# A four-layer transformer kernel: token rows go to fixed expert regions in bursts of four scatters, with gathers and maxima moved

## The chip, the cores and the metric

The kernel runs on one core of a Trainium2 chip. The metric is the device time of one execution in microseconds (us). Engines are named as the profile names them: PE (matrix products, with PEld for its weight loads), DVE (vector), ACT (activations, and one DMA queue), POOL (elementwise work and the indirect DMAs), SP (only a DMA queue).

## The reference

Eight sequences of 256 tokens with 128 features pass four layers, each added to its input. The two `ffn` layers share their weights.

```python
x = x + attn_a(layernorm(x))   # "rope": 16 heads of 8, rotated q, k, v; output rotated back
x = x + ffn(layernorm(x))      # "ffn"
x = x + attn_b(layernorm(x))   # "cov": covariance scores of centred heads
x = x + ffn(layernorm(x))      # "ffn"
# ffn(x): h = x + attention(ln1(x)); h + moe(ln2(h))
# moe(t): probs = softmax(t @ w_gate); top 2 of 8 experts, weights renormalised
#         out += we[:, None] * (gelu(t @ w1[e] + b1[e]) @ w2[e] + b2[e])     # 128 -> 512 -> 128
```

## The kernel before

All activations stay in SBUF: `X` and `Hs` (residual streams), `U` (normed input of the mixture). Two phases (`ph` 0 and 1) each hold an attention layer (rope, then cov) and an ffn layer. A phase is a software pipeline of `STEPS` = 21 steps. In step `s` six sequences are in different stages, oldest first: `u` (gate), `t` (output projection), `a` (scores and values), `m` (row maxima), `n` (projection and stacking), `p` (norm). So step 18 is the last in which scores are made, and steps 19 and 20 are drained inside the mixture. Each engine runs its own hand-written order of these parts (`step` in each engine's block); counting semaphores join them. PSUM has a ring of four banks that ACT reads (`bankE`), three that DVE reads (`bankR`) and one for values (`bankO`).

The attention part: PE makes raw scores into `bankR`, DVE takes maxima of them (`do_max`, L1109, two heads at a time), then scores go into `bankE`, ACT exponentiates (L834) and PE multiplies with the values (L466). For the rope layer DVE makes two products per tensor (`rotate`, L1093) that POOL adds (`rotated`), for keys, queries and values. POOL norms a sequence (`norm`), and stacks keys and queries in split precision (`stack_k`, `stack_q`).

The mixture: after the attention of an ffn layer, tokens are sorted by expert, in two halves of four sequences, since each token goes to two experts. DVE chooses experts (`choose`, `weigh`), PE counts (`do_rank`), and DVE works out from counts and ranks (`sort_rows`) the place of each token's two rows in a list in which each expert has whole tiles of 128 rows (`SLOT`), and each tile's expert (`EID`). A half has `NTL` = 23 tiles. POOL writes `U` to these places in DRAM (`scatter`, L1560: 16 indirect DMAs of 128 rows of 512 bytes per half, in one run: the first half's after step 18, the second's after step 20). SP loads each tile's first-layer weights (`load_w`, L393 reads the expert's number into a register, L395 loads 258 KB; seven buffers) and groups of four sorted tiles (`load_x`, L384, 256 KB; two buffers). PE turns a group (`turn_x`, L695), then for each tile multiplies into 512 hidden features (`hidden`, L707) and back (`outputs`, L720); ACT applies gelu (L951), DVE copies out (`evacuate`, L1312), ACT's queue stores to `sorted_y` (L962). Later POOL fetches each token's two rows (`gather`, L1578) into eight buffers `Yg`, and DVE adds them with their weights (`combine`, L1323). In PE's order `turn_x` of a half's first two groups stands ahead of its first `hidden`, and `hidden` runs three tiles ahead of `outputs`. `drain` puts the end of the ffn attention's work beside the tiles of the first half, and `fill` the start of the cov layer beside the second half of phase 0. Phase 1 has no `fill`: its second half is tiles alone, then gathers and the output.

Before all this SP writes zeros over `sorted_u` once (L367), since places without a token are read too.

## Time and profile before

| | |
|---|---|
| time, median of 3 runs | 901.24 us (893.77 to 902.31) |
| the profiled execution | 898.2 us, its span 896.4 us |
| granted clock of PE, mean of the span | 0.923 |
| busy: PE, PEld, DVE, ACT, POOL | 86%, 61%, 61%, 61%, 54% |
| phase 0: steps / mixture | to about 297 us / 323 to about 460 us |
| phase 1: steps / mixture, end | to about 725 us / 754 to 896 us |

A line of the profile names the source line, the engine, the operation and its operands (out<-in), how often it stands there in a row (x8), and in brackets how long the engine had been idle and what ended that. The clock is given in shares of full speed; it has two levels, 1.00 and 0.50.

### The profile page before, as it was taken

Reading aid. Unit: us, or ns where it says so; the run is one execution under the profiler, and the core shown is the slowest. Engines: PE = TensorE matmul, PEld = TensorE weight load, DVE = VectorE, ACT = ScalarE, POOL = GpSimd, SP = SyncE. Lnnn points to the kernel's source line nnn. Section 1 sums busy time; section 2 is a strip of 40 time slices with the busy share of each in tenths; the row PEclk is TensorE's granted clock in tenths of the full one; section 3 lists DMA queues with packets and bytes.
Section 4 is the critical chain, followed back from the end, with each engine's and each line's share of the span. In section 5 each row is a group of like instructions: output and inputs, shape, how many; then the busy total and the mean of one; then the engine's idle time right before and its main releaser. Section 6 shows DMA issues by size and latency. Waiting matters only on the chain.

```text
span 896.4 us, 21301 instructions
## 1 busy us (share of the span) xinstructions
PE 767.0 (86%) x7166; PEld 546.7 (61%) x7166; DVE 544.5 (61%) x1370; ACT 543.4 (61%) x1264; POOL 484.2 (54%) x906
## 2 busy tenths in 40 slices
PE   1999999999999399697988999999999948968970
PEld 1756655666565189497964565566666525958970
DVE  4699899788988123012486887878889822211232
ACT  0377777878787256154546676787877834715640
POOL 6667678747762621504645665844777273060436
PEclk9999999999999789698999899999999977978995
DMA  9300000000000436266210000000000042635842
GB/s 274 111 3 3 3 2 3 4 3 3 4 2 4 130 107 175 79 182 175 79 38 13 16 18 5 4 3 3 3 3 3 3 124 77 173 103 143 245 124 67
DMA packets 57657, 56.29 MB, mean 63 GB/s; under 512 B 6856, under 2 KB 42448, under 8 KB 57552
## 3 DMA queue, kind: packets, MB, share of 16 engines
q1 hardware_dynamic: 39200, 39.13, 15.5%
q0 software_dynamic: 4096, 8.40, 3.2%
q10 hardware_dynamic: 14256, 7.41, 2.9%
q8 instruction: 61, 1.00, 0.5%
q14 instruction: 44, 0.36, 0.1%
HBM read 40.10 MB, written 14.29 MB: 61 GB/s over the span
## 4 chain that ended last, share of the span: by engine, by line
PE 56%; DVE 21%; issue 11%; POOL 7%; DMA 3%; ACT 2%; another core or an unknown queue 0%; ACTq 0%; POOLq 0%; DVEq 0%; SPq 0%
DVE M L1109 11%; PE bankO L466 11%; PE bankR L720 8%; PE bankE L707 7%; PE bankE L485 7%; PE bankE L439 6%; DVE QKV L1071 2%; POOL Yg L1578 2%; PE bankR L452 2%; PE bankE L476 2%; PE bankR L506 2%; PE bankR L536 1%; PE bankR L738 1%; PE bankR L554 1%; DMA Yg<-sorted_y,SLOT 1%
## 5 line engine op out<-in xcount | busy, mean ns | idle before, releaser
L1109 DVE TENSOR_REDUCE M<-bankR 128x2 f32<-128x512 f32 x512 | 326.4, 684 | 62.7 <-PE bankR L452 56.9
L834 ACT ACTIVATE Pr<-bankE 128x512 f32<-128x512 f32 x512 | 277.7, 595 | 129.5 <-PE bankE L439 109.1
L466 PE MATMUL bankO<-Pr,Vx 128*32 128x256 f32 x2048 | 170.5, 406 | 18.8 <-issue 16.1
L452 PE MATMUL bankR<-KQ 32*128 32x256 f32 x1024 | 171.3, 339 | 5.0 <-DVE M L1109 2.9
L439 PEld LDWEIGHTS bankE<-KQ 32*128 32x128 f32 x1024 | 79.6, 188 | 97.1 <-issue 64.2
L439 PE MATMUL bankE<-KQ 32*128 32x256 f32 x1024 | 133.3, 335 | 0.5 <-issue 0.5
L1312 DVE COPY Yb<-bankR 128x128 f32<-128x128 f32 x92 | 26.4, 290 | 167.9 <-PE bankR L720 111.1
L452 PEld LDWEIGHTS bankR<-KQ 32*128 32x128 f32 x1024 | 110.1, 191 | 17.1 <-DVE M L1109 12.8
L951 ACT ACTIVATE G<-bankE,W 128x128 f32<-128x128 f32 x368 | 101.5, 384 | 24.8 <-PE bankE L707 14.0
L707 PE MATMUL bankE<-XTT,W 128*128 128x128 f32 x736 | 105.1, 288 | 11.4 <-issue 4.6
L1578 POOL DMA_INDIRECT Yg<-sorted_y,SLOT x64 | 62.2, 971 | 95.6 <-DMA sorted_y<-Yb 42.0
L720 PE MATMUL bankR<-w,G 128*128 x736 | 102.7, 284 | 8.6 <-issue 6.3
L1560 POOL DMA_INDIRECT sorted_u<-U,SLOT x64 | 62.2, 972 | 80.2 <-DVE past L1292 61.9
L707 PEld LDWEIGHTS bankE<-XTT,W 128*128 128x128 f32 x736 | 95.0, 201 | 16.1 <-issue 10.8
L720 PEld LDWEIGHTS bankR<-w,G 128*128 128x128 f32 x736 | 93.4, 198 | 11.4 <-issue 11.0
L828 ACT ACTIVATE KQ<-bankE 128x512 fp32r<-128x512 f32 x128 | 70.5, 605 | 24.7 <-PE bankE L485 24.4
L466 PEld LDWEIGHTS bankO<-Pr,Vx 128*32 128x32 f32 x2048 | 41.2, 110 | 55.7 <-issue 30.2
L942 ACT ACTIVATE XTT<-bankE,lncols 128x512 f32<-128x512 f32 (+1 forms) x24 | 18.3, 763 | 68.2 <-PE bankE L695 35.9
L1402 POOL TENSOR_SCALAR lnsmall<-meanvar 128x2 f32<-128x2 f32 x48 | 11.1, 232 | 83.5 <-DVE meanvar L1039 80.9
L1477 POOL CAST Kst<-QKV 128x512 fp32r<-128x512 f32 x24 | 15.7, 654 | 65.0 <-DVE QKV L1071 37.5
L485 PE MATMUL bankE<-ident_r,Kst 128*128 128x256 f32 (+1 forms) x256 | 39.9, 302 | 4.1 <-POOL Kst L1480 4.1
L1323 DVE SCALAR_TENSOR_TENSOR X<-Yg,SH,X 128x128 f32<-128x128 f32 x64 | 22.3, 362 | 33.6 <-DMA Yg<-sorted_y,SLOT 30.0
(169 smaller groups left out, 1147.0 us busy)
## 6 DMA issues: line engine op xcount, KB each, us to landing
W<-in_w1b SPq DMA_DIRECT2D x92, 258.0 KB
sorted_y<-Yb ACTq DMA_DIRECT2D x92, 64.0 KB
XT<-sorted_u SPq DMA_DIRECT2D x20, 256.0 KB
sorted_u<-Yg SPq DMA_DIRECT2D x2, 1472.0 KB, 9.7
KQ<-MT SPq DMA_DIRECT2D x128, 4.0 KB
X<-in_x SPq DMA_DIRECT2D x8, 128.0 KB, 7.3
sorted_u<-U,SLOT POOLq DMA_INDIRECT x64
Yg<-sorted_y,SLOT POOLq DMA_INDIRECT x64
```

Of the source, the lines that this page charges most:

```text
L439: k = mm(act_bank("S", layer, b, h)[:, z * T:z * T + T], KT[rows, kb, g, z * P:z * P + P], QT[rows, kb, g, :], start=True, stop=True)
L452: k = mm(dve_bank("raw", layer, b, h)[:, z * T:z * T + T], QT[rows, kb, g, z * P:z * P + P], KT[rows, kb, g, :], start=True, stop=True)
L466: k = mm(bankO[SL * j:SL * j + SL, cols], Vx[:, b % VB, kc, HG * g + j, :], Pr[:, g % 2, j, kc, :], start=(g % 2 == 0 and kc == 0), stop=( ...
L485: return mm(bank[:, i * P:i * P + n], src, ident_r[:, 0:n], start=True, stop=True)
L707: k = mm(act_bank("hid", ph, at)[:, c * P:c * P + P], W1[:, n % NW, c * P:c * P + P], XTT[:, (ph * NGRP + q) % 2, j, :], start=True, stop= ...
L720: k = mm(dve_bank("out", ph, at)[:, 0:D], G[:, (ph * NAT + at) % NGB, c, :], w2[:, bass.ds(e * FC + c, 1), :].rearrange("p o d -> p (o d)" ...
L828: return nc.scalar.activation(dst, src, ACT.Copy)
L834: nc.scalar.activation(Pr[:, (h // HG) % 2, h % HG], act_bank("S", layer, b, h).rearrange("p (k q) -> p k q", k=TT), ACT.Exp, scale=EXP_SC ...
L951: nc.scalar.activation(G[:, n % NGB, c, :], act_bank("hid", ph, at)[:, c * P:c * P + P], ACT.Gelu_apprx_tanh, bias=W1[:, n % NW, FF + c:FF ...
L1109: v.tensor_reduce(M[:, b % 2, :, h], dve_bank("raw", layer, b, h).rearrange("p (t k) -> p t k", t=TT), AX.X, ALU.max, negate=True).then_in ...
L1560: g.indirect_dma_start(sorted_u[half][:, :], bass.IndirectOffsetOnAxis(ap=SLOT[:, half, n:n + 1], axis=0), U[:, b, t, :], None).then_inc(s ...
L1578: g.indirect_dma_start(Yg[:, n % NYG], None, sorted_y[half][:, :], bass.IndirectOffsetOnAxis(ap=SLOT[:, half, at:at + 1], axis=0)).then_in ...
```

## The change

- `sorted_u` becomes one region of `CAP` = 1024 rows per expert (4 MB a half, before 1.5 MB). A token's place is then expert x 1024 + rank, and needs no total count. So places are worked out per block of two sequences (`place_rows`, four a phase) and the scatters go out in bursts of four: after steps 16, 17, 18 (two bursts, the second waits for the 14th head of the scores), after step 20, and then after tiles 5, block 3's places, and tile 14.
- Tiles are found in `sorted_u` by a start row per tile (`sort_tiles` makes `EID` and `ROW`, 13 operations, for the first half in the middle of step 18, where `sort_rows` stood at its head). `load_x` reads this row into a register and loads one tile of 64 KB: 46 loads a phase instead of 12. Their order among SP's weight loads is new: 16 ahead of a half's tiles, eight pairs beside tiles 19 to 26.
- Places in `sorted_y` are worked out separately (`place_outputs`, five operations a half).
- PE counts per block: `do_totals` and `do_rank` four times a phase each instead of twice.
- Zeros are written from `G` (cleared on POOL in step 2, 2560 columns) by ACT's queue: eight DMAs of 1 MB, one at the head of each of steps 4 to 11.
- Gathers during the cov layer: all four of a sequence at the head of POOL's step, before only one there, and the others behind `stack_k`, `stack_v` and `norm`. `gather(0, 1)` goes ahead of step 0's norm. DVE's `combine` and `norm_in` of sequences 4 to 7 go one pair of maxima earlier.
- In the rope layer a pair of maxima stands between the two products of the keys' rotation.

```diff
@@ SP @@
+            def load_x(ph, at):
+                half, i = divmod(at, NTL)
+                q, j = group_of(at)
+                k = (ph * NGRP + q) % NXG
+                r = sp.value_load(ROW[0:1, half, i:i + 1], min_val=0, max_val=E * CAP - P)
                 if i == 0:
                     sp.wait_ge(scattered[half], 16 * GROUPS * (ph + 1))
+                if j == 0:
+                    need(sp, x_turned, ph, q - NXG)
+                sp.dma_start(XT[:, k, j, :], sorted_u[half][bass.ds(r, P), :]).then_inc(x_in[k], 16)
...
                 for at in range(NW):
                     load_w(ph, at)
-                for q in range(2 * NXG):
-                    load_x(ph, q)
+                for i in range(2 * NXG * XG):
+                    load_x(ph, i)
                 for at in range(NAT):
                     if at + NW < NAT:
                         load_w(ph, at + NW)
+                    if 2 * NXG * XG <= at + 11 < NTL:
+                        load_x(ph, at + 11)
+                    if NTL - XG <= at < NTL + XG:
+                        for i in range(2):
+                            load_x(ph, NTL + 2 * (at - NTL + XG) + i)
+                    if NTL + XG <= at < NAT - 3 * XG:
+                        load_x(ph, at + 3 * XG)
@@ PE, in step; totals and ranks per block @@
+                if ends_block(gone2, 0):
+                    do_rank(*block_of(gone2))
...
+                if ends_block(gone, 1):
+                    do_totals(*block_of(gone))
@@ ACT, before a step @@
+                    if ph == 0 and 4 <= s < 12:
+                        zero((s - 4) // 4, s % 4)
@@ DVE @@
                 if rope:
                     rotate(*n, 1, 0)
-                    rotate(*n, 1, 1)
                 if m:
                     do_max(*m, 2)
+                if rope:
+                    rotate(*n, 1, 1)
...
+            def place_rows(ph, j):
+                half, at = j // 2, (j % 2) * BG
+                io = iota[:].unsqueeze(1).broadcast_to([P, BG, E])
+                need(dve, ranked, ph, j)
+                v.scalar_tensor_tensor(rank[:], io, float(CAP), dve_bank("rank", ph, j)[:, 0:BG * E].rearrange(
+                    "p (g e) -> p g e", e=E), ALU.mult, ALU.add).then_inc(placed.sem, 1)
...
+                tt(rank[:], rank[:], one_hot(j * BG, BG), ALU.mult).then_inc(placed.sem, 1)
...
+                v.tensor_reduce(place[:, at:at + BG], rank[:], AX.X, ALU.add).then_inc(placed.sem, 1)
...
+                v.tensor_copy(SLOT_U[:, half, at:at + BG], place[:, at:at + BG]).then_inc(placed.sem, 1)
@@ POOL @@
                 if fetched:
-                    gather(0, p[1] + 1, range(0, 1))
+                    gather(0, p[1] + 1)
                 if n:
                     if n == (3, 0):
                         clear_cov()
                     stack_k(*n)
-                if fetched:
-                    gather(0, p[1] + 1, range(1, 2))
...
                     if ph and s == 0:
                         gather(0, 0)
+                        need(pool, evacuated, 0, NTL + 1)
+                        gather(0, 1)
                     step(*sequences(ph, s))
...
+                    if s == 16:
+                        scatter(ph, 0, 0)
+                    if s == 17:
+                        scatter(ph, 0, 1)
+                    if s == 18:
+                        scatter(ph, 1, 0)
+                        need(pool, scores, *sequences(ph, 18)[2], 14)
+                        scatter(ph, 1, 1)
                     if s == STEPS - 1:
-                        scatter(ph, 1)
+                        scatter(ph, 2, 0)
+                        need(pool, evacuated, ph, 5)
+                        scatter(ph, 2, 1)
+                        scatter(ph, 3, 0)
+                        need(pool, evacuated, ph, 14)
+                        scatter(ph, 3, 1)
```

## Rows read from the trace of the kernel before

**Rows 1.** The page: granted clock in 40 slices, and the chain by engine.

```profile
PEclk9999999999999789698999899999999977978995
...
PE 56%; DVE 21%; issue 11%; POOL 7%; DMA 3%; ACT 2%; another core or an unknown queue 0%; ACTq 0%; POOLq 0%; DVEq 0%; SPq 0%
```

**Rows 2.** Windows: start:end, length, busy of PE, PEld, DVE, ACT, POOL; clock; DMA.

```profile
302.00:314.00 12.00, 1.30 (x13) 0.40 (x16) 0.00 (x0) 1.29 (x3) 7.69 (x8) 0.50 0.31 93
350.00:356.00 6.00, 6.00 (x57) 5.91 (x56) 3.54 (x15) 2.85 (x9) 1.10 (x1) 1.00 0.78 205
362.00:380.00 18.00, 10.05 (x32) 7.26 (x31) 1.47 (x4) 2.62 (x9) 9.63 (x11) 0.60 0.22 66
400.00:410.00 10.00, 10.00 (x92) 10.00 (x91) 2.03 (x7) 5.88 (x20) 3.84 (x4) 1.00 0.88 247
792.00:812.00 20.00, 10.87 (x38) 8.45 (x38) 1.76 (x5) 2.96 (x10) 10.74 (x12) 0.59 0.22 65
```

**Rows 3.** Timeline of POOL, first and last of phase 0's first 16 scatters.

```profile
291.77 1.23 POOL L1560 DMA_INDIRECT sorted_u<-U,SLOT  x1 [2.23 <-DVE past L1292]
...
311.04 0.96 POOL L1560 DMA_INDIRECT sorted_u<-U,SLOT  x1 [0.30 <-issue]
```

**Rows 4.** Waits from 285 to 325 us: total, times, longest.

```profile
DVE Hs L1130 <- remote: 15.1, 1, 15.1
```

**Rows 5.** Timeline of POOL, the last of the first four gathers.

```profile
404.99 0.95 POOL L1578 DMA_INDIRECT Yg<-sorted_y,SLOT  x1 [0.31 <-issue]
```

**Rows 6.** Timeline of SP, merged: loads of weights, x7 and x8.

```profile
293.31 13.42 SPq L395 DMA_DIRECT2D W<-in_w1b  x7
...
722.04 12.05 SPq L395 DMA_DIRECT2D W<-in_w1b  x7
...
824.10 8.10 SPq L395 DMA_DIRECT2D W<-in_w1b  x8
```

**Rows 7.** Timeline of PE at the first tiles of each phase.

```profile
321.38 1.91 PE L695 MATMUL bankE<-ident,XT 128*128 128x128 f32 x8
323.31 3.55 PE L707 MATMUL bankE<-XTT,W 128*128 128x128 f32 x24
...
754.08 3.22 PE L707 MATMUL bankE<-XTT,W 128*128 128x128 f32 x24
```

**Rows 8.** DMA issues: size, us from issue to landing.

```profile
sorted_u<-Yg SPq DMA_DIRECT2D x2, 1472.0 KB, 9.7
...
ident<-in_ident ACTq DMA_DIRECT2D x1, 64.0 KB, 3.0
```

**Rows 9.** Timeline of DVE, the end of sort_rows, phase 0, first half.

```profile
292.12 0.18 DVE L1297 TENSOR_SCALAR EID<-npast 128x23 uint32<-128x23 f32 x1
```

**Rows 10.** SP's register and row loads: nanoseconds min/median/max, first and last start.

```profile
L393 SPq TENSOR_LOAD <-EID x92: 3/271/700, 292.3 to 852.8; - x92
...
L384 SPq DMA_DIRECT2D XT<-sorted_u x24: 359/382/503, 313.3 to 840.9; - x24
```

**Rows 11.** Timeline of PE, end of phase 1's first half.

```profile
814.27 1.06 PE L707 MATMUL bankE<-XTT,W 128*128 128x128 f32 x8
...
816.06 1.06 PE L707 MATMUL bankE<-XTT,W 128*128 128x128 f32 x8
...
823.27 2.50 PE L707 MATMUL bankE<-XTT,W 128*128 128x128 f32 x20 [0.43 <-ACT XTT L942]
```

**Rows 12.** Timeline of DVE, combine of sequence 1.

```profile
418.52 0.35 DVE L1323 SCALAR_TENSOR_TENSOR X<-Yg,SH,X 128x128 f32<-128x128 f32 x1 [6.68 <-DMA Yg<-sorted_y,SLOT]
```

**Rows 13.** Timelines of POOL and PE in a cov step with gathers.

```profile
495.71 0.99 POOL L1578 DMA_INDIRECT Yg<-sorted_y,SLOT  x1
...
500.85 0.68 PE L485 MATMUL bankE<-ident_r,Zhl 128*128 128x256 f32 x4 [1.20 <-POOL Zhl L1443]
```

**Rows 14.** Timelines of PE and POOL in a rope step.

```profile
105.87 0.44 PE L546 MATMUL bankE<-ident,O 128*128 128x128 f32 x2
...
104.58 0.79 POOL L1536 TENSOR_TENSOR O<-O 128x256 f32<-128x256 f32 x1
```

More of the change, by code:

```diff
@@ L690, in turn_x @@
             def turn_x(ph, q):
                 x = ph * NGRP + q
-                pe.wait_ge(x_in[x % NXG], 16 * (x // NXG + 1))
+                pe.wait_ge(x_in[x % NXG], 16 * sum(GROUP[y % NGRP][1] for y in range(x % NXG, x + 1, NXG)))
                 ring_e.take(pe, ("x", ph, q))
@@ L1182, in step @@
                     do_fold()
+                if ends_block(gone, 1):
+                    weigh(*block_of(gone))
+                if a and LAYERS[a[0]] == "ffn" and a[1] == NB - 1:
+                    sort_tiles(a[0] // 2, 0)
                 if m:
@@ L1186, in step @@
                     rotate(*n, 0, 0)
+                if late(p):
+                    combine(0, p[1])
+                    norm_in(*p)
                 if m:
@@ L1200, in step @@
                     rotate(*n, 2, 1)
+                if ends_block(gone, 1):
+                    copy_totals(*block_of(gone))
                 if u:
                     do_gate(*u)
-                if block_of(gone) is not None:
+                if ends_block(gone, 0):
                     weigh(*block_of(gone))
@@ L1211, in step @@
                     norm3_in(*t)
+                if ends_block(gone, 0):
+                    copy_totals(*block_of(gone))
+                if ends_block(gone, 1):
+                    place_rows(*block_of(gone))
             def choose(ph, j):
@@ L1334, in drain @@
                     weigh(ph, 3)
+                if i == 0:
+                    place_rows(ph, 2)
                 if i == 9:
-                    copy_totals(ph, 1)
+                    copy_totals(ph, 3)
                 if i == 10:
-                    sort_rows(ph, 1)
+                    place_rows(ph, 3)
+                if i == 11:
+                    sort_tiles(ph, 1)
+                if i == 13:
+                    place_outputs(ph, 1)
                 if i in (15, 19):
@@ L1365, in mixture @@
                 add_b2(ph, 1)
+                place_outputs(ph, 0)
+                copy_totals(ph, 2)
                 residual(layer, NB - 1)
```

208 lines of the change are left out of this document (114 added, 94 removed).

## The prediction, made before the changed kernel was run

> **What bounds the kernel now.** I read the page first, then windows, then each engine's timeline where the windows show a hole. The chain of work puts 56% on PE and 21% on DVE [rows 1]: in the attention steps PE is the engine that is nearly always busy. But 11% is "issue", time in which nothing that the profile shows was waited for, and the clock row has its dents in slices 14 to 18 and 34 to 37, around the mixtures [rows 1]. The windows show what stands there. From 302 to 314 us PE makes 13 matmuls, and from 362 to 380 us 32, where 57 fit into the 6 us from 350 to 356 us; phase 1 has the same hole at 792 to 812 us, with 38 [rows 2]. In these stretches PE, DVE and ACT all stand nearly still, and the DMA engines too are mostly idle (share 0.22 to 0.31), so it is neither bandwidth nor one late engine. POOL alone works evenly: it issues 16 scatters, from 291.77 to 312.0 us, one each 1.27 us [rows 3]. The wait of DVE for the output projection is put down to "remote", with no engine to name, 15.1 us in one piece [rows 4], though PE had made that product long before. I call this a crawl. There are four, one for each half and phase. Each begins some 5 us after the first scatter of a run (four or five scatters) and ends 2 to 4 us after its last. Four gathers in a row (ending at 405.9 us) do nothing of the kind: PE is busy for all of 400 to 410 us, with 92 matmuls, beside DMA engines at 0.88 [rows 2, 5].
>
> So the first question for the change is whether bursts of four scatters stay below what starts a crawl; the second is what comes late once the crawls are gone. The sum is made against the profiled execution, 898.2 us (span 896.4 and 1.8 around it). That lies 3.0 us under the median of the three runs and inside their spread.
>
> **1. The crawls beside the tiles (second half's scatters), removed.** 362 to 380 us holds 32 matmuls; at 57 per 6 us these are 3.4 us of work, so 14.6 us are lost; 792 to 812 us holds 38, that is 4.0 us, so 16.0 us are lost [rows 2]. Together -30. In the new order these 16 scatters go out as 4, 4, 4 and 4, held apart by the waits for tile 5, for block 3's ranks (tile 10) and for tile 14; at 1.8 us a tile [rows 11] the gaps are 4 us or more between bursts of 5 us, except the last with some 2 to 3 us. Nobody waits behind POOL there: its next work is the gathers. The bound from the other side is 0, if four are too many already (rival 1).
>
> **2. The start of each mixture.** Now the first tile's product begins 30.0 us after SP's first weight load in phase 0 (293.31 to 323.31) and 32.0 us after it in phase 1 (722.04 to 754.08) [rows 6, 7]. Two things fill this: the crawl, and the sorted rows, which SP can ask for only when the 16 scatters have landed (first row load at 313.3) [rows 10]. After the change the rows have long been scattered, and the crawl should be shorter. What is late next is SP's own queue. Undisturbed, it needs 8.10 us for eight weight loads, 1.10 us from one to the next [rows 6]; most of it is reading the register, checking it and forming the address. The new `load_x` has all of that, so I take 1.10 us for it as well. It could be nearer to the 0.38 us of a plain row load [rows 10] (lower bound, with something for the address 0.5), or to the 1.9 us each of the seven loads in a crawl (13.42 us for 7, upper bound) [rows 6]; the undisturbed row is the nearest in kind. PE turns two groups, eight tiles, before the first product, so 7 + 8 loads must be issued: 14 x 1.10 = 15.4, landing 3.0 as the 64 KB load of `ident` [rows 8], turn and copy 1.3 [rows 7]: 19.7 us. The first load also starts later: the tile numbers came at 292.3 us [rows 9], and `sort_tiles` now stands behind `divide` in step 18 and waits for 13 operations, which I put at 3.3 us. That is 23.0 against 30.0 and 32.0: -7 and -9, together -16. The two bursts of step 18 stand only about 1 us apart (heads 1 to 14 of the scores are done nearly when the first burst is), so they make a run of eight, half of one that crawled; I give back +4 for a rest of the crawl. Bounds: 0 and +14.
>
> **3. The boundary between the halves, a new wait.** The sixteen rows' loads of the second half are issued in pairs beside the weight load of tiles 19 to 26, and the one of tile 19 waits for that tile's gelu. PE needs eight of them before product 23: four rounds of three issues, 12 x 1.10 = 13.2 us, begun 2.6 us after product 19 starts (my estimate: 1.06 for its matmuls and somewhat more for its four activations), plus 3.0 landing and 1.0 for the turns is 19.8 us. PE itself is there sooner: product 22 to product 23 takes 7.2 us now, and three tiles of 1.8 to 1.9 us lie between 19 and 22, together 12.8 us [rows 11]. SP is therefore some 6 to 7 us late, in each phase; less 0.5 for what overlaps: +12 for both. Queued behind on SP are the weight loads 27 to 33, which have seven buffers of slack (13 us). In the second half SP needs 3.3 us a tile for four tiles and 2.2 for seven against 1.8 of PE [rows 11]; the slack takes most of this, and I put +3 for both phases (phase 1 above all, phase 0 has the cov work beside it). Lower bound 0, upper +12.
>
> The register load is where a rule speaks against the change. The row has 271 ns at the median [rows 10]. The Trainium skill, in DMA: Bandwidth & Descriptors, section Latency and other measured facts, gives `tensor_load` a floor of about 600 ns. By that an issue would take some 1.43 us, and by the 52 issues that count (14 twice, 12 twice) the whole would come out 17 us longer, at 890. The trace's 271 ns decides for me.
>
> **4. More small work.** Beside the tiles PE has a few more matmuls of counting and DVE one more `copy_totals` and `place_rows` and five operations of `place_outputs`, each of 0.2 to 0.3 us like the sort's [rows 9]: +2.4 for both phases. In steps 15 to 18 DVE gets two `copy_totals` and two `place_rows` and PE the matching matmuls, each holding one of three banks until DVE reads it: +2 a phase, +4 (0 to +6).
>
> **5. Gathers.** In phase 0 DVE waits 6.68 us for sequence 1's rows at 418.52 [rows 12], with the copies of tiles queued behind it, since the gathers stand behind the norm on POOL. Now they follow the first four at once (the norm's statistics come later anyway). PE loses less than DVE does, as it waits for the norm at the same time: -4. In cov steps 4 to 7 the loop combine, norm, projection, stacking, next combine sets the pace: a gather at 495.71 stands right ahead of the norm, another between `stack_k` and `stack_q`, and PE stands 1.20 us before it can turn the norm's result [rows 13]. At the head all four take 5.1 us (4 x 1.27) and fit into the time in which POOL waits for the projection. About one gather and a part of the pair of maxima, 1.2 to 1.5 us, a step in four steps: -5 (-8 to 0).
>
> **6. Rope order.** The keys' second product comes one pair of maxima (1.2 us) later. POOL's sum, keys and then the rotation back follow. It ends at 105.37 us and PE uses it at 105.87 [rows 14]: 0.5 us of slack against 1.2 us, so up to 0.7 us a step is lost, while raw scores find free banks sooner. I put +2 for eight steps (-2 to +6).
>
> **7. Zeros.** Eight DMAs of 1 MB when nothing else moves; 1472 KB took 9.7 us [rows 8], so one is done in about 6 us of a 16 us step. The small moves of maxima share the engines with it, and ACT's queue issues it ahead of its exponentials, 0.4 us or so by SP's plain loads [rows 10]; clearing `G` keeps POOL for a while in the second step, of which I have no row: +2 (0 to +8).
>
> The sum: -30 - 16 + 4 + 12 + 3 + 2.4 + 4 - 4 - 5 + 2 + 2 = -25.6, so 898.2 - 25.6 = 872.6, rounded to 873.
>
> **Rivals.** (1) Bursts of four crawl too, or the crawl belongs to each scatter and is only moved. For it: I see only the onset after four or five, not what builds up; step 18 has eight in a row. Against it: PE keeps its pace for the first 5 us of each run. If half of the 30 and the 12 of terms 1 and 2 is gone, it is 873 + 21 = 894. (2) Slower than before: SP's queue becomes the bound, since each tile now needs two register-addressed issues. 52 issues stand in the path, so the time is 873 + 52 x (issue - 1.10); with the 1.9 us of the crawl rows [rows 6] it is 915, and it decides against the change from 1.6 us an issue on. For it: both rates are in the trace. Against: the slow one stands only in crawls. (3) No late SP: row loads cost about 0.5 us, or their order hides them. Then term 3 is 0 and term 2 gains 8 x 0.6 twice: 873 - 15 - 10 = 848. For it: plain loads are that cheap. (4) The change doesn't do what it says: the crawls come from the weight loads beside the scatters. Against it: no weight load is in flight through most of 362 to 380 us (DMA share 0.22) [rows 2]. It would give 898 + 15 = about 905, as the new costs stay.
>
> **How the numbers follow.** The forecast gets 0.60, rival 1 0.13, rival 2 0.07, rival 3 0.17, rival 4 0.03. The forecast's own terms reach from 860 to 886. The range goes from 848 (rival 3) to 896 (rival 1). A measurement of this kernel can tell about 1% (9 us) from no change. Faster by over 1%: the forecast, rival 3 and a part of rivals 1 and 2, 0.84; within 1% 0.10; slower by over 1% 0.06.
>
> **What would show it.** Windows of six us beside the scatters with PE at its 9 matmuls a us, and no wait of over 5 us put down to "remote". SP's queue with 15 issues in a row before the first turn, 1.1 us apart, and PE's first product 19 to 20 us after the first weight load. A wait of PE for `XT` ahead of product 23 in both phases. In cov steps 4 to 7 no wait of PE for `Zhl`. The prediction would be wrong if a crawl stands behind bursts of four, or if SP's pace isn't 1.1 us.

## The result and the profile after

The changed kernel takes **912.4 us** (median of 4 runs, 906.49 to 916.20) against 897.5 us for the kernel before (4 runs, 893.74 to 902.31): a ratio of 1.016, 95% interval 1.012 to 1.020. It is slower, and the forecast was 873 with a range of 848 to 896. The profiled execution of the changed kernel ("after") took 906.49 us, its span is 904.6, that is 8.2 more than before. It is the fastest of the four, 5.9 us under their median, so the traces hold 8.2 of the 14.9 us between the medians. Ratios leave out an execution over 1.5% above the fastest of its kernel, of which there are two below: 913.16 of b_small, the one that was profiled, and 889.11 in the second series of c_best.

The first three views are those of [rows 1] and [rows 2]. The page's row of the granted clock, and its chain by engine:

```profile
PEclk9799999999998589989987999999999857898995
...
PE 49%; DVE 20%; issue 8%; POOL 7%; SPq 5%; ACT 4%; another core or an unknown queue 3%; DMA 3%; ACTq 0%; POOLq 0%; DVEq 0%
```

The dip beside phase 0's tiles (slice 17) is filled, and those ahead of the mixtures (slices 14 and 33) are deeper, 5 where they were 7. SP's queue, 0% of the chain before, is 5%. Windows of after (start:end, length, busy of PE, PEld, DVE, ACT, POOL, then clock and DMA):

```profile
285.00:315.00 30.00, 28.21 (x176) 14.53 (x175) 12.05 (x56) 13.54 (x30) 10.80 (x16) 0.50 0.22 64
302.00:314.00 12.00, 12.00 (x75) 5.99 (x77) 4.56 (x30) 6.70 (x14) 4.24 (x5) 0.50 0.40 115
350.00:356.00 6.00, 3.28 (x20) 3.12 (x20) 2.29 (x23) 5.04 (x16) 0.09 (x1) 0.78 0.55 149
362.00:380.00 18.00, 16.78 (x143) 15.84 (x143) 6.19 (x26) 9.71 (x35) 7.51 (x8) 1.00 0.61 175
400.00:410.00 10.00, 7.75 (x66) 7.22 (x65) 0.58 (x2) 3.45 (x12) 7.11 (x8) 1.00 0.57 151
792.00:812.00 20.00, 19.02 (x157) 18.34 (x158) 7.07 (x31) 8.93 (x30) 7.65 (x8) 0.96 0.59 164
```

The change does what it says: 362 to 380 us holds 143 matmuls where there were 32, and 792 to 812 us 157 where there were 38 [rows 2]. But 350 to 356 us, quiet before with 57, has 20 now (the tail of the second burst of four, whose last scatter is issued at 349.13 us), and 400 to 410 us has 66 in place of 92 (eight gathers in a row). And from 285 to 315 us PE is busy for 28.2 of 30 us at a granted clock of 0.50. The kernel before has its low clock there too, but for a shorter time and in a crawl (engines nearly still beside a run of scatters, as the prediction has it), where PE had little to do. Its window:

```profile
300.00:318.00 18.00, 6.44 (x39) 2.86 (x40) 2.05 (x13) 2.83 (x7) 11.05 (x15) 0.53 0.35 108
```

Where the 8.2 us come from is best seen as stretches between landmarks that both kernels have. In this table "14" and "15" are the first exponentials of the 15th and 16th sequence of a phase, h0, h22, h23 and h45 the `hidden` products of those tiles; every number is a difference of two start times in the timelines, of one execution each; "single" is a_single. The last four columns are experiments, told below.

| us | before | after | difference | before, no scatters | after, no scatters | single | n_totals |
|---|---|---|---|---|---|---|---|
| start to 14 | 272.1 | 273.4 | +1.3 | 269.6 | 272.5 | 277.0 | 272.5 |
| 14 to 15, phases 0 / 1 | 13.5 / 13.5 | 22.5 / 23.0 | **+18.5** | 13.5 / 13.5 | 20.4 / 20.6 | 19.5 / 19.3 | 15.5 / 15.5 |
| 15 to h0 | 37.8 / 39.7 | 30.9 / 31.6 | **-15.0** | 19.9 / 20.7 | 29.3 / 29.6 | 32.3 / 32.6 | 28.2 / 28.0 |
| h0 to h22 | 62.0 / 62.0 | 52.5 / 55.6 | **-15.9** | 44.8 / 46.6 | 46.9 / 47.6 | 46.8 / 47.6 | 46.5 / 47.6 |
| h22 to h23 | 7.2 / 7.2 | 13.3 / 13.6 | **+12.5** | 7.2 / 7.2 | 13.2 / 13.5 | 17.6 / 17.1 | 13.2 / 13.4 |
| h23 to h45 | 57.3 / 39.7 | 58.1 / 43.6 | +4.7 | 56.2 / 39.7 | 58.4 / 43.7 | 59.4 / 44.3 | 58.4 / 45.6 |
| h45 to phase 1's 14 | 251.0 | 253.0 | +2.0 | 250.6 | 252.8 | 254.5 | 252.4 |

The differences add up to 8.1. Timeline of PE, first in step 18, then at the first and the second start of phase 0's tiles:

```profile
288.18 0.99 PE L592 MATMUL bankR<-w_gate,UT 128*128 128x8 f32 x4 [1.79 <-DVE totals L1313]
...
325.80 1.12 PE L728 MATMUL bankE<-ident,XT 128*128 128x128 f32 x4 [3.58 <-DMA XT<-sorted_u]
326.70 3.51 PE L740 MATMUL bankE<-XTT,W 128*128 128x128 f32 x18
...
391.56 1.12 PE L728 MATMUL bankE<-ident,XT 128*128 128x128 f32 x4 [4.45 <-DMA XT<-sorted_u]
```

The wait for `totals` is new; phase 1 has it too, 1.79 us at 718.92. PE's ring of banks for DVE has three. The block's totals take one between pairs 4 and 5 of raw scores, pair 5 takes the other two, and the gate's product must wait until DVE, which does maxima pair 5 first, has copied the totals. The other two waits are the prediction's: rows that SP has asked for too late. SP's own timeline:

```profile
307.80 7.67 SPq L412 DMA_DIRECT2D W<-in_w1b  x7
316.25 12.84 SPq L402 DMA_DIRECT2D XT<-sorted_u  x12
...
384.24 0.33 SPq L412 DMA_DIRECT2D W<-in_w1b  x1
385.32 1.43 SPq L402 DMA_DIRECT2D XT<-sorted_u  x2
387.51 0.33 SPq L412 DMA_DIRECT2D W<-in_w1b  x1
```

Twelve row loads in 12.84 us (11 distances and 0.3), and a round of one weight load and two row loads every 3.27 us (384.24 to 387.51): 1.14 and 1.09 us an issue, for the 1.10 forecast. (The view ends at 330 us; in all 16 row loads follow each other.) The first weight load stands at 307.80 since the tile numbers are late. Timeline of DVE, the last place of block 1, and the division for which `sort_tiles` waits:

```profile
295.89 0.17 DVE L1333 CAST SLOT_U<-place 128x8 uint32<-128x8 f32 x1
...
303.49 0.36 DVE L1163 RECIPROCAL rden<-bankR 128x32 f32<-128x32 f32 x1 [6.16 <-PE bankR L555]
...
306.62 0.18 DVE L1366 TENSOR_SCALAR ROW<-row 128x23 uint32<-128x23 f32 x1
```

The counts were there at 296 us, and DVE stood 6.16 us for PE's turn of `OT`, in PE's order at half clock. The two bursts of step 18, which the prediction had about 1 us apart, stand 6.36 us apart. Timeline of POOL, the first scatter of the second:

```profile
308.77 0.95 POOL L1653 DMA_INDIRECT sorted_u<-U,SLOT_U  x1 [6.36 <-PE bankE L458]
```

### The profile page after: what moved, and what is told of

It reads as the page before. It is cut to its first block, busy times and chain, and to the rows that moved or that the text cites. A ratio compares the mean times of both kernels' runs of the same rounds, so it can differ in the third digit from the quotient of the medians.

```text
span 904.6 us, 21975 instructions
## 1 busy us (share of the span) xinstructions
PE 788.0 (87%) x7190; PEld 558.8 (62%) x7190; DVE 552.4 (61%) x1430; ACT 544.3 (60%) x1264; POOL 486.1 (54%) x906
## 4 chain that ended last, share of the span: by engine, by line
PE 49%; DVE 20%; issue 8%; POOL 7%; SPq 5%; ACT 4%; another core or an unknown queue 3%; DMA 3%; ACTq 0%; POOLq 0%; DVEq 0%
DVE M L1153 10%; PE bankO L485 9%; PE bankE L504 7%; PE bankE L458 6%; PE bankE L740 6%; PE bankR L753 6%; PE bankR L471 3%; ACT G L985 2%; DVE QKV L1115 2%; PE bankE L495 2%; SPq L397 2%; PE bankR L555 2%; SPq L402 1%; PE bankR L573 1%
## 5 line engine op out<-in xcount | busy, mean ns | idle before, releaser
L471 PE MATMUL bankR<-KQ 32*128 32x256 f32 x1024 | 176.2, 341 | 7.9 <-DVE M L1153 4.1
L485 PE MATMUL bankO<-Pr,Vx 128*32 128x256 f32 x2048 | 175.6, 418 | 0.3
L458 PEld LDWEIGHTS bankE<-KQ 32*128 32x128 f32 x1024 | 83.1, 195 | 102.9 <-issue 65.7
L458 PE MATMUL bankE<-KQ 32*128 32x256 f32 x1024 | 138.4, 345 | 0.9 <-issue 0.6
L985 ACT ACTIVATE G<-bankE,W 128x128 f32<-128x128 f32 x368 | 100.6, 383 | 38.1 <-PE bankE L740 27.6
L1672 POOL DMA_INDIRECT Yg<-sorted_y,SLOT_Y x64 | 61.5, 961 | 104.1 <-DVE Yb L1398 46.2
L740 PE MATMUL bankE<-XTT,W 128*128 128x128 f32 x736 | 107.8, 296 | 8.7 <-ACT G L985 7.2
L1653 POOL DMA_INDIRECT sorted_u<-U,SLOT_U x64 | 62.6, 978 | 90.8 <-DVE SLOT_U L1333 44.7
L740 PEld LDWEIGHTS bankE<-XTT,W 128*128 128x128 f32 x736 | 98.8, 210 | 11.5 <-issue 10.1
L753 PE MATMUL bankR<-w,G 128*128 x736 | 100.3, 280 | 4.3 <-issue 2.5
L485 PEld LDWEIGHTS bankO<-Pr,Vx 128*32 128x32 f32 x2048 | 42.0, 112 | 37.8 <-issue 15.9
L976 ACT ACTIVATE XTT<-bankE,lncols 128x512 f32<-128x512 f32 (+1 forms) x24 | 18.3, 760 | 54.8 <-PE bankE L728 45.1
L504 PEld LDWEIGHTS bankE<-ident_r,Kst 128*128 128x128 f32 x256 | 35.3, 206 | 8.1 <-POOL Kst L1571 4.7
```

Source lines behind the costliest of these rows:

```text
L458: k = mm(act_bank("S", layer, b, h)[:, z * T:z * T + T], KT[rows, kb, g, z * P:z * P + P], QT[rows, kb, g, :], start=True, stop=True)
L471: k = mm(dve_bank("raw", layer, b, h)[:, z * T:z * T + T], QT[rows, kb, g, z * P:z * P + P], KT[rows, kb, g, :], start=True, stop=True)
L485: k = mm(bankO[SL * j:SL * j + SL, cols], Vx[:, b % VB, kc, HG * g + j, :], Pr[:, g % 2, j, kc, :], start=(g % 2 == 0 and kc == 0), stop=( ...
L504: return mm(bank[:, i * P:i * P + n], src, ident_r[:, 0:n], start=True, stop=True)
L740: k = mm(act_bank("hid", ph, at)[:, c * P:c * P + P], W1[:, n % NW, c * P:c * P + P], XTT[:, (ph * NGRP + q) % 2, j, :], start=True, stop= ...
L753: k = mm(dve_bank("out", ph, at)[:, 0:D], G[:, (ph * NAT + at) % NGB, c, :], w2[:, bass.ds(e * FC + c, 1), :].rearrange("p o d -> p (o d)" ...
```

## The experiments

Each run has the kernel before beside it on its chip; "interval" is the 95% interval of the ratio to it. The runs form five series, each on one chip: experiments 1 and 3; 2, a_oldgath and c_best; 4, 5, 6 and b_small; b_gathers, b_rope, a_store and c_store; c_best and c_store again. The kernel before has medians of 896.5 to 900.4 us in them. The changed kernel was in none of them, so a difference to its 912.4 us, or between two series, is across chips and is read with its stretches in the table. The kernels without scatters leave the sorted rows unmoved (the tiles then compute on zeros) and drop the waits for them.

### 1. No scatters, in both kernels

```diff
-                for n in range(GROUPS):
+                for n in ():
```

b_noscat is the kernel before:

> The kernel before, with its 64 scatters left out (the sorted rows stay zero, so the mixtures compute on zeros); everything else, the waits apart, is as before. Theory R (a run of more than four indirect DMAs slows every engine): all four stretches of few matmuls go, 4 x some 13 to 16 us less what SP's queue makes late in their place: 845 to 860 against 897. Theory W (weight loads beside them slow the engines): the stretches stay, 885 to 897.

a_noscat is the changed one:

> The changed kernel, with its 64 scatters left out. Theory S (each burst of four still makes the engines stumble for some us, and in steps 17 and 18 the clock falls with it): exponentials of sequence 7 begin 13 us after those of sequence 6 as before, no 30 us of half clock, about 30 us less than the changed kernel's 912, so 880 or less. Theory Q (the delay in steps 17 and 18 comes from the counting matmuls and totals in the ring of banks): that delay stays, and the time falls by less than 10 us.

Measured: **b_noscat 827.6** (ratio 0.920, interval 0.916 to 0.924) and **a_noscat 887.0** (0.986, 0.981 to 0.990). Scatters cost the kernel before 70 us and more (897.5 to 899.7 with them), twice the crawls that I had priced beside the tiles. The changed one loses only 25 us to them, so that part of the change is worth some 45 us. But all the rest of it costs 59 us. The table above says where, phases 0 and 1 together, for 54 of them: 14.0 in "14 to 15", 18.3 in "15 to h0", 3.1 beside the first half's tiles, 12.3 at the boundary, 6.2 in the second halves. The same window in both (the first is b_noscat's, the second a_noscat's, 3 us shorter):

```profile
285.00:315.00 30.00, 29.06 (x261) 21.55 (x262) 11.72 (x56) 21.24 (x55) 7.74 (x19) 1.00 0.50 141
```

```profile
285.00:312.00 27.00, 26.60 (x168) 13.62 (x169) 11.12 (x58) 12.06 (x25) 3.62 (x9) 0.51 0.21 60
```

PE is busy nearly all the time in both, but with 261 matmuls in one and 168 in the other. One has the high level of its clock and the other the low; the work differs too, as b_noscat has its first tiles from 302.98 us on. So no scatter is needed for step 18 to be slow. Of the expectations, b_noscat has none of theory R's stretches, and gains more than its 845 to 860. In a_noscat theory Q's delay stays (20.4 us where theory S has 13), but the scatters cost 25 us and not under 10.

### 2. How many scatters in a row make a crawl

The kernel before with only the first 4 or 8 of each run of 16 (the rest of the rows isn't moved):

```diff
-                for n in range(GROUPS):
+                for n in range(4):          # b_eight: 8
```

> The kernel before with only the first 4 of each run of 16 scatters (three quarters of the rows aren't moved). Without any it is 827.6, with all 16 about 898. Theory onset, as the prediction has it: a run of four is over before a crawl starts, so 828 to 832. Rival proportion: every scatter costs the whole chip some 1.1 us (72 us for 64), wherever it stands in a run: 16 of them give 845.

> The same with the first 8 of each 16. Theory onset: four of each eight fall into the crawl, and twelve of each sixteen did before: a third of the 70 us, 851. Rival proportion: half of them, 863.

Measured: **b_four 835.7** (interval 0.925 to 0.936), **b_eight 866.8** (0.957 to 0.974). From none to 4, 8 and 16 of each run the time goes 827.6, 835.7, 866.8, some 898: for 16, 16 and 32 scatters more 8, 31 and 31 us, that is 0.5, 1.9 and 1.0 us each. Beside the tiles alone (h0 to h22) it goes 44.8, 45.2, 53.2, 62.0 in phase 0, and 46.6, 46.9, 54.6, 62.0 in phase 1. So there is an onset between the fourth and the eighth, and a lone run of four costs tiles 0.3 to 0.5 us. Right behind step 18 it costs more: "15 to h0" is 21.0 and 25.3 us, where it is 19.9 and 20.7 without scatters. The prediction's onset holds beside the tiles, but not as a rule for the whole time: 835.7 lies above the 828 to 832 of theory onset, and 866.8 is nearer to the rival's 863 than to its 851.

### 3. Scatters one by one, and the first half's late

a_single: each scatter of the changed kernel waits for a head of the scores, or a tile, of its own.

```diff
                 for n in range(part * BG // 2, part * BG // 2 + BG // 2):
+                    need(pool, *paced[n % (BG // 2)])
...
-                    scatter(ph, 2, 0)
-                    need(pool, evacuated, ph, 5)
-                    scatter(ph, 2, 1)
+                    scatter(ph, 2, 0, [(evacuated, ph, x) for x in (1, 2, 3, 4)])
+                    scatter(ph, 2, 1, [(evacuated, ph, x) for x in (5, 6, 7, 8)])
```

> The changed kernel, each scatter by itself, paced by heads of the scores (two heads apart, some 2 us) and by tiles (one apart). Theory R (what counts is the length of an unbroken run): the stumbles at the end of each burst vanish, 885 to 895. Rival (each scatter costs the other engines a fixed time, however spaced): no better than 912.

a_late0: the four bursts of the first half all stand behind step 18, where the kernel before has them.

> The changed kernel, with the first half's four bursts all issued after step 18, as before. Theory S: steps 17 and 18 lose their 11 us of delay a phase, and a crawl like the old one stands at the start of the mixture instead; about 5 to 15 us less than 912. Theory Q: the delay in steps 17 and 18 stays, and the old crawl comes on top: 5 to 20 us more than 912.

Measured: **a_single 899.5** (0.9965 to 1.001), 13 us under the changed kernel, and **a_late0 927.0** (1.023 to 1.034), 15 over it. The first lies between theory R (885 to 895) and its rival, the second where theory Q had it (5 to 20 over 912), with step 18 still slow (20.3 and 20.7 us). In the table a_single's tiles take what they take without scatters (46.8 and 47.6 against 46.9 and 47.6): paced by tiles, 32 scatters cost nothing there. The bursts of four cost 52.5 - 46.9 and 55.6 - 47.6, together 13.6 us. More than half of phase 0's 5.6 us (3.2, at tiles 11 and 12) stands behind the second burst, where DVE's and PE's short steps of counting follow each other. The bursts stand 5.8, 11.8 and 3.1 us apart (POOL's timeline). Four of them cost 5.6 and 8.0 us and b_four's one 0.3 to 0.5, and no run says whether that is their succession or the work that they stand beside. Windows of 350 to 360 us in after, a_single and a_noscat:

```profile
350.00:360.00 10.00, 7.28 (x50) 6.83 (x49) 3.17 (x26) 6.02 (x19) 0.09 (x1) 0.83 0.55 149
```

```profile
350.00:360.00 10.00, 8.96 (x77) 8.50 (x77) 3.85 (x26) 7.87 (x25) 1.91 (x2) 1.00 0.59 160
```

```profile
350.00:360.00 10.00, 10.00 (x92) 9.91 (x91) 5.25 (x26) 5.44 (x18) 0.00 (x0) 1.00 0.68 183
```

a_single pays elsewhere: its last scatter stands at 376 us, behind h22, and SP asks for the second half's rows only when all have landed, so h22 to h23 grows by 4.3 and 3.5 us. a_late0 has "15 to h0" at 40.2 and 41.4, as before the change: the early bursts are what shortens it.

### 4. The totals' wait in step 18

n_totals is a_noscat with DVE's copy one pair earlier:

```diff
+                if ends_block(gone, 1):
+                    copy_totals(*block_of(gone))
                 if m:
                     do_max(*m, 5)
...
-                if ends_block(gone, 1):
-                    copy_totals(*block_of(gone))
```

> The changed kernel without its scatters, as a_noscat (886.96), and in step 18 DVE copies the totals one pair of maxima earlier, ahead of pair 5 and not behind it. Theory ring: in a_noscat PE stands 1.79 us before the gate product at 285.40, since the totals hold a third bank until DVE has done pair 5, and from then on the granted clock is 0.50 for some 28 us. Without that wait the clock stays at 1.00 through step 18, which then ends as in b_noscat, some 7 to 9 us earlier in each phase: 868 to 873. Rival counting: the work of counting and placing itself is what makes step 18 longer, and the clock falls anyway at the next small gap: only the two waits of 1.8 us go, 883.

Measured: **876.1** (0.974 to 0.983), 10.9 under a_noscat (11.8 between the profiled executions), between the two. "14 to 15" falls from 20.4 and 20.6 to 15.5 and 15.5, which is 10.0 of the 11.8, though the two waits themselves are 3.6. The kernel of experiment 5, in the series of n_totals and without this edit, has 20.4 and 20.6 again. What goes beyond the waits goes with the clock: here is the same place in a_noscat and in n_totals.

```profile
285.40 0.83 PE L592 MATMUL bankR<-w_gate,UT 128*128 128x8 f32 x4 [1.79 <-DVE totals L1313]
```

```profile
283.80 0.48 PE L592 MATMUL bankR<-w_gate,UT 128*128 128x8 f32 x3
```

And two windows of n_totals:

```profile
285.00:292.00 7.00, 5.71 (x72) 3.24 (x68) 4.37 (x15) 4.36 (x9) 2.98 (x7) 1.00 0.01 4
292.00:304.00 12.00, 12.00 (x76) 6.35 (x68) 4.29 (x29) 6.99 (x15) 0.00 (x0) 0.51 0.32 87
```

Without the wait the clock stays at 1.00 until 292 us; in a_noscat it falls at 285.6 (0.90 from 284 to 286), as the wait ends. It falls in n_totals all the same, 2 us behind another wait of PE (1.13 us at 290.18), and this the ring theory had not foreseen.

The changed kernel itself has the same wait, but there the clock is down before it. The wait begins at 286.39 and 717.13, and two windows of after put the fall at 285.1 and 715.2 us:

```profile
284.00:286.00 2.00, 1.79 (x12) 1.12 (x12) 1.34 (x3) 2.00 (x7) 0.00 (x0) 0.78 0.00 0
714.00:716.00 2.00, 1.70 (x16) 0.88 (x8) 1.82 (x3) 2.00 (x6) 0.00 (x0) 0.80 0.00 0
```

Ahead of the fall stands a wait of 1.06 us for maxima (at 282.82), beside step 17's burst. No run moves the copy alone with scatters present. What there is: "14 to 15" is 19.3 to 20.7 us in a_single and a_late0, and 15.5 to 19.2 in the four executions of experiment 8 with single scatters and the early copy.

### 5. The price of a row load

n_const is a_noscat with fixed row numbers (so the tiles get other rows):

```diff
-                r = sp.value_load(ROW[0:1, half, i:i + 1], min_val=0, max_val=E * CAP - P)
-                sp.dma_start(XT[:, k, j, :], sorted_u[half][bass.ds(r, P), :]).then_inc(x_in[k], 16)
+                sp.dma_start(XT[:, k, j, :], sorted_u[half][i * P:i * P + P, :]).then_inc(x_in[k], 16)
```

> The changed kernel without its scatters, as a_noscat (886.96), and the loads of sorted rows take fixed places in place of a row number read into a register (so the tiles get other rows). Theory register: eight such loads stand ahead of each half's first product; at about 0.45 us in place of 1.10 they come 5 us earlier at each of the four starts, less what the weight loads keep: 868 to 874. Rival placement: the order of SP's queue and the wait for the gelu of tile 19 set the start, not the cost of one issue: 880 to 885.

Measured: **868.2** (0.960 to 0.971), 18.8 under a_noscat (15.2 between the profiled executions), as theory register has it. SP's timeline at the boundary:

```profile
367.55 0.35 SPq L411 DMA_DIRECT2D W<-in_w1b  x1
367.94 0.91 SPq L401 DMA_DIRECT2D XT<-sorted_u  x2
369.60 0.35 SPq L411 DMA_DIRECT2D W<-in_w1b  x1
```

A round takes 2.05 us (367.55 to 369.60) in place of 3.27, so reading, checking and adding the row number is 0.61 us a load. The starts gain 2.8 and 3.6 us (26.5 and 26.0), the boundaries 3.9 and 4.6 (9.3 and 8.9), phase 1's second half 4.5 (39.2, as in the kernel before). The Trainium skill's `tensor_load` floor of about 600 ns, cited ahead (DMA: Bandwidth & Descriptors, section Latency and other measured facts), is the better guide to this price than the row's 271 ns [rows 10], but it comes within the 1.10 us and not on top of it, so the 890 worked out by it was not the way it came out.

### 6. One group ahead of the first tile

a_turn1 turns the second group of each half behind the first tile's product:

```diff
-                    turn_x(ph, half * NGRP // 2 + 1)
                     for at in range(half * NTL, half * NTL + LEAD):
                         hidden(ph, at)
+                        if at == half * NTL:
+                            turn_x(ph, half * NGRP // 2 + 1)
```

> The changed kernel with its scatters (912.4), where PE turns the second group of a half behind the first tile's product, not ahead of it. So the first product needs four row loads in place of eight. Theory SP's queue: four issues of 1.10 us less stand ahead of each of four starts, of which the next tiles take a part back as they need rows 5 to 8: -8 to -16, that is 896 to 904. Rival crawl: PE stands there because the whole chip crawls behind the scatters, and the rows would be there: 908 to 912.

Measured: **900.5** (1.0015 to 1.0065), 11.9 under the changed kernel. "15 to h0" is 27.6 and 28.1 (3.3 and 3.5 less), h22 to h23 8.9 and 7.3 (4.4 and 6.3 less): four issues of 1.1 us at each of four starts, 17.5 us together. The tiles behind the starts give back 9.6 of it (h0 to h22 is 56.6 and 55.3, h23 to h45 61.1 and 46.4), and between the profiled executions 4.5 us are left. The median lies in the theory's 896 to 904. SP's queue is what PE waits for at the starts.

### 7. The small parts

b_small puts the gathers at the head, the earlier combine and the rope order into the kernel before; b_gathers and b_rope are its two parts; a_oldgath takes gathers and combine back in the changed kernel.

```diff
-                    gather(0, p[1] + 1, range(0, 1))
+                    gather(0, p[1] + 1)            # b_gathers, b_small
...
                     rotate(*n, 1, 0)
-                    rotate(*n, 1, 1)
                 if m:
                     do_max(*m, 2)
+                if rope:
+                    rotate(*n, 1, 1)               # b_rope, b_small
```

> The kernel before with three small parts of the change alone: all four gathers of a sequence at the head of the covariance steps, the combine of sequences 4 to 7 one pair of maxima earlier, and the pair of maxima between the two products of the keys' rotation. By the terms of the prediction -5 and +2, so 897 beside 900. Rival: the covariance steps are bound by PE and DVE's own work and these change nothing, within 2 us of before. Rival two: the maxima between the rotation's products make PE wait each step, +5 to +8.

> The kernel before with all four gathers of a sequence at the head of the cov steps and the combine one pair of maxima earlier. By the prediction's term -5 (893 to 895). If the gathers are what made b_small slow, as its trace has it (from sequence 17 on the cov steps are 4 to 7 us later), +5 to +8.

> The kernel before with the pair of maxima between the two products of the keys' rotation alone. By the prediction's term +2 (902). If it is what made b_small slow, +8 (905 to 908). In b_small's trace the rope steps were 1.6 us longer in all: +1 to +2.

> The changed kernel (912.4) with all gathers of the cov layer and the combine of sequences 4 to 7 back where they stood before, gather(0, 1) behind the norm too. By the prediction's terms it would lose 9 us: 921. Theory from the traces (eight gathers in a row crawl at 408 to 413 us, and the small parts alone made the kernel before 8 us slower): the old places are better by 4 to 8 us: 904 to 908.

Measured: **b_small 905.5** beside 897.0 (1.004 to 1.011), **b_gathers 900.1** beside 896.5 (1.002 to 1.007), **b_rope 897.9** (0.9999 to 1.0035), **a_oldgath 909.5** (1.009 to 1.022), 3 under the changed kernel. None shows the gain of 5 or 9 us that term 5 has, nor does a_oldgath show the 4 to 8 us of its own theory: its ratio of 1.015 is after's 1.016. b_rope's interval holds both its +2 and nothing. In after the waits of PE for `Zhl` [rows 13] are indeed gone (0.2 us of 4.9 left; 500.79 without a wait), but from the cov layer's first to its eighth sequence it takes 127.4 us, against 126.5 before, 126.8 in b_gathers, and 126.5 in a_oldgath, where 6.1 us of these waits are back. That wait was slack. In the fill the eight gathers (400.76 to 410.5 us) make a crawl of their own. Timeline of POOL and DVE in after:

```profile
400.76 0.99 POOL L1672 DMA_INDIRECT Yg<-sorted_y,SLOT_Y  x1 [26.29 <-DMA sorted_y<-Yb]
...
412.18 0.49 DVE L1398 COPY Yb<-bankR 128x128 f32<-128x128 f32 x2 [9.81 <-remote]
```

b_small's ratio is 1.0075, its parts' are 1.0044 and 1.0017: together they fall into its interval, so nothing shows that it loses more than they do. Its profile, on which the expectation of b_gathers leans, is of its slowest execution, 913.16 us.

### 8. Stores, and all repairs together

The first row above also shows the first gather waiting for the first half's last stores, which ACT issues behind the copies of the second half's first rows. a_store issues them ahead:

```diff
+                    if half:
+                        for at in range(NTL - LAG, NTL):
+                            store(ph, at)
                     for x in range(2):
                         copy_x(ph, half * NGRP // 2 + x)
                         hidden(ph, half * NTL + x)
```

> The same edit in the changed kernel (912.4), where the first gather stands at 400.8 us and eight gathers in a row crawl at 408 to 413. Theory stores: gathers from about 385 us, beside the wait for the second half's rows, where PE has nothing to lose: -5 to -10, 902 to 907. Rival: the crawl of the eight gathers only moves onto the boundary and makes SP's row loads later still: 910 to 914.

c_best is the changed kernel with single scatters, totals copied earlier, one group ahead, and the old places of gathers and combine; c_store is c_best with the early stores. Both ran twice, in two series.

> The changed kernel with four edits together: each scatter by itself, paced by heads and tiles (alone 13 us less), totals copied ahead of maxima pair 5 (11 us less where there were no scatters), the second group turned behind the first tile (12 us less), and the old places of gathers and combine (4 to 8 us less). If the costs are separate, their sum gives 870. If the totals' wait and the row loads are hidden by what is left of the crawls, the single terms shrink by half: 885. If gathers in their old places bring nothing, 876.

> The combination c_best (885.96), and ACT issues the stores of the first half's last tiles ahead of the copies of the second half's first rows, not behind them. Theory stores: the first gather, at 399.8 us there, comes some 8 to 10 us earlier, combine and norm of the cov layer with it, the 8.5 us wait at tile 36 goes: -5 to -9, 877 to 881. Rival: the fill is bound by the loop of combine, norm and projection on DVE and POOL whenever it starts: 884 to 887.

> c_best once more, beside c_store on one chip. If the 14 us between them came from the clock and the chip and not from the stores, the two now differ by 2 to 6 us. If the edit is worth 14 us, 886 against 872 again. In the first case the profile's step 18 of phase 0 may come out either way: end of scores at about 288 or at about 298 us.

> c_store once more, beside c_best on one chip. By the traces the edit alone brings 2 to 3 us at the boundary and perhaps as much in phase 1; by the medians of the first runs it brings 14.

Measured: **a_store 904.8** (1.006 to 1.012); **c_best 886.0** (0.980 to 0.991), then **876.8** (0.971 to 0.979); **c_store 871.8** (0.971 to 0.977), then **882.3** (0.978 to 0.983). The first gather does come earlier (373.32 us in c_store, 9.8 us behind h22; 399.80 in c_best, 24.7 behind it), but side by side on one chip c_store was 5 us behind c_best. a_store lies in its theory's 902 to 907, 8 us under the changed kernel but across chips, and its profiled execution of 911.91 us is its slowest. The stores bring nothing that these runs can show. The combination beats both kernels, by 1.5 to 2.6% the one before. c_best's expectations had 870, 876 or 885, and its two series lie at two of them. What it varies by shows in two executions of the same c_best, of 892.0 and 871.8 us. First step 18 and what follows:

```profile
288.00:316.00 28.00, 27.96 (x184) 14.62 (x188) 12.86 (x53) 14.84 (x32) 10.26 (x15) 0.55 0.22 64
```

```profile
288.00:316.00 28.00, 20.83 (x177) 11.71 (x170) 12.94 (x66) 13.88 (x28) 16.77 (x29) 0.82 0.35 101
```

In the second the stretch is nearly over with 7 us of PE idle at a clock of 0.82; in the first PE needs it all at 0.55. "14 to 15" is 18.8 in one and 15.7 in the other. But 7.0 of the 20.2 us between them stand in the rope layer, where the kernel has no scatters, again at two clocks (c_best's 892.0 us first):

```profile
42.00:153.00 111.00, 103.45 (x1000) 65.52 (x1003) 94.09 (x192) 78.35 (x157) 77.09 (x143) 0.92 0.13 53
```

```profile
42.00:153.00 111.00, 103.33 (x1079) 64.65 (x1078) 99.62 (x205) 83.18 (x167) 82.41 (x151) 0.98 0.15 59
```

## Why the prediction was wrong

By its own terms, against the stretches of the table (one execution of each kernel; term 5's -4 in the fill falls into the row of the second halves):

| term | predicted | traces |
|---|---|---|
| 1, with 2.4 of 4: beside the first halves' tiles | -27.6 | -15.9 |
| 2: start of the mixtures | -12 | -15.0 |
| 3: boundary / second halves | +12 / +3 | +12.5 / +4.7 |
| 4: steps 15 to 18 | +4 | **+18.5** |
| 5: gathers | -9 | +2.0 |
| 6 and 7: rope order, zeros | +4 | +1.3 |
| sum | -25.6 | +8.1 |

The two sums are 33.7 us apart: 14.5 of it is term 4, 11.7 term 1, 11.0 term 5, and the others take 3.5 back. The remaining 5.9 of the 39.4 us between 873 and 912.4 are the profiled execution's distance from its median.

**The step that failed first is term 4**, "two `copy_totals` and two `place_rows` ... +2 a phase". I costed the instructions and named the resource (one of three banks until DVE reads it), but not what stands behind it on PE, nor what a gap does to the clock. Of the 18.5 us, 10.0 go with the place of one copy where there are no scatters (experiment 4), 4.0 are left in n_totals (15.5 against 13.5 in each phase), and 4.5 come with the scatters (22.5 and 23.0 against 20.4 and 20.6). So step 18 lengthens without any scatter, and the copy's place decides most of that. How the 18.5 us divide between the totals' wait and the earlier fall of the clock in the changed kernel itself stays open. It is a cost that a new use of a ring brings: no price of an instruction shows it.

**Term 5 had the wrong sign of evidence.** I took a wait of PE for the norm as the pace of the cov steps; it went and the pace stayed. And the onset after four or five scatters stood in my own text, but I didn't apply it to the eight gathers in a row that the change makes, as I had seen four gathers do nothing. Taking the gathers back didn't make the changed kernel faster by a clear amount, so what they cost stays open; that they don't gain is shown.

**Term 1 was right in mechanism and mis-sized**: lone runs of four are nearly free (experiment 2) and the old crawls beside the tiles were 17.2 and 15.4 us (62.0 - 44.8, 62.0 - 46.6), against the 14.6 and 16.0 read from the windows. The four bursts of each half give back 13.6 of these 32.6, nearly the 15 that rival 1 takes from term 1. Its 6 us of term 2 did not come: that term is -15.0 for -12, and the run of eight in step 18, for which it had set +4, never formed, as the wait for head 14 held its halves 6.36 us apart. The new work beside the tiles is 3.1 us for 2.4.

**Terms 2 and 3 held**: 1.1 us an issue, 18.9 us from the first weight load to the first product (307.80 to 326.70; 19.8 in phase 1, from 738.40 to 758.22) for 19.7, and SP late by 6 us at each boundary (experiments 5 and 6). Rival 3 is refuted by this, rival 2's slow issue never came, and rival 4 falls with experiment 1. No rival had the cause that decided: that rival 2's 915 is near the outcome is chance, as its slow issue isn't there. Terms 6 and 7 did better than the pair of traces says: the changed kernel and the kernels made from it reach their 15th sequence at 272.3 to 279.4 us, 275.0 on average, the old order of this part at 269.6 to 272.1, 270.8 on average, which is about +4. The range's upper end was rival 1 (894 by its own sum, 896 in the range), and the outcome needed rival 1 and a step 18 of which no case told.

## What to carry to other kernels

When a change puts a new product into a ring of banks, write out the ring's order around it: who waits for the bank it takes, and what that engine does first. Two gaps of 1.8 us on PE went with 10 us of longer steps here, where the granted clock fell behind them and the work that followed was PE's alone. Pace indirect transfers by the consumer's own progress rather than cut a run into bursts: beside the tiles bursts of four won back 19.0 of 32.6 us, single scatters all of it. A wait in the trace that a change removes is worth nothing until the stretch around it is known to be set by it.

## What the runs showed of the hardware

- **Time at half clock is not time lost.** (1 - mean clock) x 2 x span is the time at half clock: 138 us before, 168 after, 139 in a_noscat, 101 in n_totals, 53 in b_noscat. Before and a_noscat have the same and differ by 14 us. The two executions of c_best had 162 and 104 us of it and differed by 20 us. The Trainium skill (TensorE: Matmul & The Clock Gate, section HAM oscillation) reckons the cost as half of such time, by which it would be 29, an estimate; the measured 20 is less.
- The clock stayed low while PE was busy nearly without a break: 28.2 of 30 us in after's first window. What brings it back there, the runs don't show.
- A run of indirect transfers from POOL slows every engine once it is longer than four to eight: shown for scatters by experiment 2 (tiles of 45.2 us beside four, 53.2 beside eight, 62.0 beside sixteen). Eight gathers stand beside the same in one window (66 matmuls where there were 92), but no run takes them alone. The same 32 scatters cost the tiles nothing when nearly each waited for a tile of its own (a_single).
- Medians of one kernel differ by 9 and 10 us from one series to the other (c_best 886.0 and 876.8, c_store 871.8 and 882.3), more than the interval of one series says; the kernel before stays within 4. Differences of up to 10 us to a changed kernel of another series are to be read so, and those of 11 to 13 (a_turn1, n_totals, a_single) rest on their stretches more than on their medians.
